# The attention loop of a Perceiver block in another order: TensorE takes Wo behind the keys and turns xn behind the values, and VectorE, ScalarE and POOL are reordered to match

## The reference

```python
def _L0_attn_ref(x, wq, bq, wk, bk, wv, bv, wo, bo):     # x is layer-normed
    q = proj(wq, bq); k = proj(wk, bk); v = proj(wv, bv)   # 16 heads of 16
    scores = jnp.einsum('bhqd,bhkd->bhqk', q, k) / np.sqrt(hd)
    attn = jax.nn.softmax(scores, axis=-1)
    o = jnp.einsum('bhqk,bhkd->bhqd', attn, v)
    align = jnp.sum(o * v, axis=-1, keepdims=True) / (v_norm_sq + EPS)
    o = o - align * v                                      # what lies along v is taken off
    return jnp.einsum('bsd,ed->bse', o, wo) + bo
...
x = x + _L0_xattn_ref(_layernorm(x), ctx_768, ...)
x = x + _L0_attn_ref(_layernorm(x), ...)
x = x + _L0_ffn_ref(_layernorm(x), ...)                    # argmax of 14 logits picks the expert
```

## Time and profile before

| what | us |
|---|---|
| median of 3 runs | 520.83 |
| lowest and highest | 520.41, 521.19 |
| the profiled execution | 520.4 |
| its span, first to last instruction | 518.4 |
| TensorE busy | 500.3 (97%) |
| VectorE, ScalarE busy | 344.8, 346.8 (67%) |
| POOL busy | 241.5 (47%) |
| granted TensorE clock, mean | 0.994 |

### The profile page before, as it was taken

How to read it: one execution, slowest core, us unless ns; L and a number is a source line. 1 busy time by engine, 2 the same in 40 slices (tenths; PEclk the granted TensorE clock), 3 DMA queues, 4 the chain that set the end, 5 groups by cost and what they waited for, 6 DMA issues and landing times.

```text
span 518.4 us, 14286 instructions
## 1 busy us (share of the span) xinstructions
PE 500.3 (97%) x4324; PEld 397.8 (77%) x4325; DVE 344.8 (67%) x1022; ACT 346.8 (67%) x837; POOL 241.5 (47%) x406
## 2 busy tenths in 40 slices
PE   8999999999999999999999999999999999999993
PEld 6554555566788788887878888778989999999992
DVE  4578666646788988898898989997553333323231
ACT  3777777668988888889888888887453334343430
POOL 2366555336434555564555546552753333333332
PEclk9999999999999999999999999999999999999997
DMA  8964446200001122212231111146667766666620
GB/s 299 368 198 150 157 157 209 63 1 1 2 3 38 45 86 93 92 54 84 93 91 50 58 61 60 45 135 206 191 200 236 215 216 204 224 182 216 192 82 10
DMA packets 30497, 65.68 MB, mean 127 GB/s; under 512 B 4640, under 2 KB 18594, under 8 KB 30448
## 3 DMA queue, kind: packets, MB, share of 16 engines
q1 hardware_dynamic: 26560, 55.99, 34.6%
q0 software_dynamic: 3456, 8.85, 4.4%
q10 hardware_dynamic: 432, 0.26, 0.2%
HBM read 54.21 MB, written 11.60 MB: 127 GB/s over the span
## 4 chain that ended last, share of the span: by engine, by line
PE 86%; DVE 5%; issue 4%; ACT 1%; POOL 1%; DVEq 0%; ACTq 0%; POOLq 0%
PE psum L1387 12%; PE psum L1400 11%; PE psum L1322 9%; PE psum L1273 6%; PE psum L1160 6%; PE psum L1281 5%; PE psum L1335 5%; PE psum L1294 5%; PE psum L1241 5%; PE psum L1203 3%; PE psum L1210 3%; PE psum L1172 3%; PE psum L1186 3%; PE psum L1214 3%; PE psum L1175 3%
## 5 line engine op out<-in xcount | busy, mean ns | idle before, releaser
L1387 PEld LDWEIGHTS psum<-arena,ring 128*128 128x128 f32 x640 | 77.3, 192 | 3.5 <-issue 1.7
L1387 PE MATMUL psum<-arena,ring 128*128 128x128 f32 x640 | 78.2, 275 | 0.9 <-ACT arena L1104 0.7
L1400 PE MATMUL psum<-w_s,arena 128*128 x320 | 75.9, 381 | 0.0
L924 DVE TENSOR_TENSOR arena<-psum,tok 128x256 f32<-128x256 f32 x40 | 17.0, 424 | 84.9 <-PE psum L1400 83.2
L1098 ACT ACTIVATE arena<-psum 128x256 f32<-128x256 f32 x40 | 15.4, 385 | 85.9 <-PE psum L1160 58.7
L1400 PEld LDWEIGHTS psum<-w_s,arena 128*128 128x128 f32 x320 | 57.8, 190 | 6.4
L483 POOL TENSOR_TENSOR ov<-o_n,v_s 128x256 f32<-128x256 f32 x32 | 23.5, 733 | 74.9 <-DVE o_n L693 74.9
L1068 ACT ACTIVATE arena<-kT,head_mask 128x256 f32<-128x256 f32 x128 | 57.4, 500 | 0.0
L541 POOL DMA_INDIRECT out<-arena,token_of x40 | 40.0, 999 | 19.0 <-POOL token_of L533 13.9
L1104 ACT ACTIVATE arena<-psum,b_s 128x128 f32<-128x128 f32 x160 | 45.6, 375 | 4.0 <-PE psum L1387 2.2
L795 DVE TENSOR_REDUCE smax<-psum 128x16 f32<-128x1024 f32 x32 | 39.1, 1221 | 4.8 <-PE psum L1294 4.4
(11 more groups left out here) (193 smaller groups left out, 1119.9 us busy)
## 6 DMA issues: line engine op xcount, KB each, us to landing
ring<-w SPq DMA_DIRECT2D x40, 512.0 KB, 3.7
w_s<-ctxT SPq DMA_DIRECT2D x15, 768.0 KB, 4.6
w_s<-w SPq DMA_DIRECT2D x16, 448.0 KB, 3.6
slot_rec<-routed SPq DMA_DIRECT2D x40, 132.0 KB, 3.5
tok<-x SPq DMA_DIRECT2D x16, 256.0 KB, 4.8
routed<-pad_rec SPq DMA_DIRECT2D x1, 1980.0 KB, 10.7
tok<-b SPq DMA_DIRECT2D x14, 128.0 KB, 3.0
out<-arena,token_of POOLq DMA_INDIRECT x40
```

The lines of the kernel that those rows point to most:

```text
L1387: mm = pe.matmul(hid_bank(p)[:, f * P:(f + 1) * P], w1_s[:, r, c * F + f * P:c * F + (f + 1) * P], xgT[:, p, c * P:(c + 1) * P], start=c = ...
L1400: mm = pe.matmul(bank(2 + q, D), hidT[:, q, f * P:(f + 1) * P], w2_s[:, bass.ds(e * (FC * D) + f * D, D)], start=f == 0, stop=f == FC - 1)
```

## The change

TensorE's step becomes: keys, Wo of tile `w`, queries, turn the probabilities, values, turn xn, scores, weighing, turn the output. Wo moves from the end of step `i - 1` to behind the keys of step `i`. Its tile is the same, and so is what it waits for. xn is turned between values and scores, where it stood between weighing and Wo, and the output is turned last. These are rows of a step of TensorE in the loop, first before, then after. `xnT,wk_s` are the keys, `xnT,wq_s` the queries, `av_s,xnT` the values, `arena,qT` the scores, `arena` 64x34 the weighing.

POOL adds the bias between `ov` and `along`, and in the loop `settled` comes ahead of `along`. ScalarE copies the queries ahead of the probabilities, and a step's end becomes: first half of the values, `oT`, the exponential, second half of the values. The diff, its core:

```diff
@@ gpsimd attention_step
                     pool.tensor_tensor(ov[:, :], o_n[:, :], v_s[:, (k - 3) % 4, :], ALU.mult).then_inc(s["ov_ok"], 1)
+                if live(i):
+                    need(pool, s["xn_ok"], i + 1)
+                    pool.tensor_tensor(rows(i), rows(i), bo_s[:, :], ALU.add).then_inc(s["bo_added"], 1)
+                if not isinstance(x, int):
+                    settled(x, (k - 9) % RING)
                 if live(y):
                     need(pool, s["coef_ok"], y + 1)
...
-                if not isinstance(x, int):
-                    settled(x, (k - 9) % RING)
-                if live(i):
-                    need(pool, s["xn_ok"], i + 1)
-                    pool.tensor_tensor(rows(i), rows(i), bo_s[:, :], ALU.add).then_inc(s["bo_added"], 1)
@@ scalar attention_step
-                if live(v):
-                    copy_probabilities(v, p)
-                if live(z) and k % GROUP == 0:
-                    route_exponents(z)
                 if live(i):
                     need(act, s["s_psum"], i - 1)
...
                     last.then_inc(s["q_ok"], 1)
-                if live(y):
-                    copy_output(y, (k - 3) % 2)
+                if live(v):
+                    copy_probabilities(v, p)
+                if live(z) and k % GROUP == 0:
+                    route_exponents(z)
...
                     spread_keys((2, 3)).then_inc(s["kd_ok"], 1)
                 if live(u):
+                    spread_first_values(u, (k - 1) % 2, (k - 1) % 4)
+                if live(y):
+                    copy_output(y, (k - 3) % 2)
+                if live(u):
                     exponentiate(u, (k - 1) % 2)
                 if live(u):
-                    spread_values(u, (k - 1) % 2, (k - 1) % 4)
+                    spread_second_values((k - 1) % 2, (k - 1) % 4)
@@ tensor attention_step
                 if isinstance(i, int) and i == NT:
                     before_scores()
                     all_scores()
+                    need(pe, s["l1_ok"], i)
+                    project(w, p)
                     return
...
                     need(pe, s["xT_ok"], i + 1)
                     need(pe, s["q_ok"], i)
...
+                    project_tile(wk_s, 0)
+                if live(w):
+                    need(pe, s["l1_ok"], i)
+                    project(w, p)
+                if live(i):
+                    project_tile(wq_s, 1).then_inc(s["qk_psum"], 1)
                 before_scores()
...
-                if ramp:
+                if live(t):
                     need(pe, s["xn_ok"], t + 1)
                     need(pe, s["xT_ok"], t)
+                    need(pe, s["oT_ok"], w + 1)
                     turn(bank(5), xn[:, 1 - p, :], s["xT_psum"])
                 if live(v) and ramp:
                     turn_probabilities(v, p)
                 all_scores()
-                if live(y):
-                    need(pe, s["xT_ok"], i + 1, NT)
-                    turn_output(y, (k - 3) % 2)
...
                     weigh_values(v, p)
-                if live(t) and not ramp:
-                    need(pe, s["xn_ok"], t + 1)
-                    need(pe, s["xT_ok"], t)
-                    need(pe, s["oT_ok"], y + 1)
-                    turn(bank(5), xn[:, 1 - p, :], s["xT_psum"])
                 if live(y):
-                    need(pe, s["l1_ok"], i + 1, NT)
-                    project(y, (k - 3) % 2)
+                    need(pe, s["xT_ok"], i + 2, NT)
+                    turn_output(y, (k - 3) % 2)
```

More of the change, by code:

```diff
@@ L701, in attention_step @@
                     dve.tensor_reduce(lmax[:, :], logit[:, :, :], AX.X, ALU.max).then_inc(s["lmax_ok"], GROUP)
+                if "weighing" in aside:
+                    aside["weighing"]()
                 if live(w):
                     need(dve, s["stats3_raw"], w + 1)
[L705 to L711, removed]
[L712 to L716 removed]
+                if live(y):
+                    need(dve, s["ov_ok"], y + 1)
+                    dve.tensor_reduce(dot[:, :], ov[:, :].rearrange("p (h d) -> p h d", h=NH), AX.X, ALU.add)\
+                        .then_inc(s["dot_ok"], 1)
+                if gather:
+                    need(dve, s["lmax_ok"], of_group)
+                    dve.tensor_tensor(lc[:, :, :], logit[:, :, :], each(lmax[:, :]), ALU.subtract)\
+                        .then_inc(s["lc_ok"], GROUP)
+                if live(y):
+                    need(dve, s["dot_ok"], y + 1)
+                    need(dve, s["rvv_ok"], y + 1)
+                    dve.tensor_tensor(coef[:, :], dot[:, :], rvv[:, (k - 3) % 4, :], ALU.mult).then_inc(s["coef_ok"], 1)
+                if settle:
+                    need(dve, s["ranked_ok"], of_last)
+                    dve.tensor_reduce(rank[:, :], ranked[:, :, :], AX.X, ALU.add).then_inc(s["rank_ok"], GROUP)
                 if scales:
@@ L725, in attention_step @@
                         .then_inc(s["ranked_ok"], GROUP)
-                if gather:
-                    need(dve, s["lmax_ok"], of_group)
-                    dve.tensor_tensor(lc[:, :, :], logit[:, :, :], each(lmax[:, :]), ALU.subtract)\
-                        .then_inc(s["lc_ok"], GROUP)
                 if sums:
@@ L775, in attention_step @@
                         .then_inc(s["pos_ok"], GROUP)
+                if gather:
+                    need(dve, s["cand_ok"], of_group)
+                    dve.tensor_reduce(arg[:, :], cand[:, :, :], AX.X, ALU.min).then_inc(s["arg_ok"], GROUP)
                 if shares:
@@ L778, in attention_step @@
                     dve.reciprocal(rec[:, done, R_PROB], lsum[:, :]).then_inc(s["prob_ok"], GROUP)
+                if live(u):
+                    need(dve, s["vv_ok"], u + 1)
+                    dve.tensor_reduce(vvsum[:, :], vv[:, :, :], AX.X, ALU.add).then_inc(s["vvsum_ok"], 1)
+                if gather:
+                    need(dve, s["arg_ok"], of_group)
+                    dve.tensor_tensor(onehot[:, :, :], experts, each(arg[:, :]), ALU.is_equal)\
+                        .then_inc(s["onehot_ok"], GROUP)
+                if live(t) and not (isinstance(t, int) and t in (1, 2)):
+                    normalise(t, (k + 1) % 2)
+                if isinstance(i, int) and i == 0:
+                    normalise(2, 0)
+                if isinstance(i, int) and i == -1:
+                    normalise(1, 1)
+                if live(w):
+                    dve.bn_aggr(rec[:, r, R_MEAN:R_MEAN + 2], stats3[:, :]).then_inc(s["stats3_ok"], 1)
+                if live(y):
+                    need(dve, s["along_ok"], y + 1)
+                    need(dve, s["oT_psum"], y - 1)
+                    dve.tensor_tensor(o_f[:, (k - 3) % 2, :], o_n[:, :], along[:, :], ALU.subtract).then_inc(s["of_ok"], 1)
                 if live(i):
```

86 lines of the change are left out of this document (33 added, 53 removed).

## The result

| what | before | after |
|---|---|---|
| median, us | 521.01 (6 runs, 520.33 to 521.52) | 532.90 (6 runs, 531.67 to 535.03) |
| ratio to before | | 1.0236, 95% interval 1.0221 to 1.0252 |
| profiled execution, its span | 520.4, 518.4 | 533.59, 531.7 |
| granted TensorE clock, mean | 0.994 | 0.992 |

The changed kernel is 2.4% slower, 532.9 us where 531.0 (524 to 535) was forecast. On the page of after, TensorE's busy time is 3.6 us more than in the earlier trace rows; VectorE's and ScalarE's hardly move, POOL's is 2.6 less. So of the 13.3 us, 9.7 are idle time of TensorE.

The account below looks back on a forecast made before the run. TensorE, busy 97% of the span, was taken as the bound. Added waits of 14.8 us less 4.5 and 0.2 removed made it net 10.1 us slower: 530.5, with the median 0.4 higher 531 us, range 524 to 535.

Parts of the forecast that it names:

- The `o_f` waits go: TensorE's nine waits for VectorE's `o_f` in the whole run all vanish: minus 4.5 us.
- xn becomes the bound: TensorE waits for VectorE's late xn: 2.0, 8.0 and 1.3 us in steps 4-11, loop, 28-29; expected sign 25 to 30 places.
- By kind of step: Loop waits for xn: 0.13 us in ordinary steps (k = 2), 0.60 in gather steps (k = 3), 0.69 at k = 0, 0.58 at k = 1.
- rival 2: At k = 1 POOL's `along` goes ahead of xn: 0.45 us more in each of four steps; 534 us, chance 0.16.
- VectorE waits out POOL's instruction: An xn beside POOL's `along` ends only behind it, about 4.46 instead of 4.24 us on the step's clock.
- A change of order removes none of these: TensorE's own work in an attention step, 7.30 us, stays; reordering only removes or makes waits.
- The loop and the steps written out: Added waits for xn: 8.0 us in loop tiles 12 to 27, 2.0 in steps 4 to 11, 1.3 in 28 and 29.
- Step 30: The slot plan delays x3, so values wait 1.1 us and xn 1.0 more: 2.1 in place of 1.3.
- The end: Last step's scores wait 1.0 us more for tile 30's shifted scores, plus 0.4 for Wo(28) being later: 1.4 added.
- The ramp stays: Ahead of the loop, the first probabilities still wait for the same exponential, so nothing is added.
- Priced at nothing: Waits for the exponential (covered by 0.3 us) or oT, and POOL's moved bias addition, were taken to cost nothing.
- Rival 4: A wash: waits for xn come to a third, 4 us, cancelling the `o_f` gain; 521 us, chance 0.04.

Follow-up runs that it names:

- a1_xn_early: Changed kernel with VectorE forming xn right behind the wait for the statistics, ahead of `dot` and the routing: 521.98 us, ratio to before 1.0021.
- b2_along_thin: Changed kernel with POOL forming only one column of 16 per head of `along`, so results differ from the reference: 537.03 us, ratio to before 1.0163.
- a3_fill: Changed kernel with seven unread matmuls added in the pause ahead of the scores of tile 31: 540.35 us, ratio to before 1.0215.
- a2_end: Changed kernel with Wo of tile 28 ahead of the scores again in the last attention step: 539.24 us, ratio to before 1.0213.
- a4_pool_old: Changed kernel with POOL's old order, `along` ahead of the `settled` waits and bias addition: 535.26 us, ratio to before 1.028.
- c0_after: Changed kernel without any edit, run again as partner on a chip where the kernel before took 528.24 us: 541.43 us, ratio 1.0259.
- b3_turn_later: Changed kernel with TensorE turning xn behind the scores instead of ahead of them: 525.25 us, ratio to before 1.0093.

## Why the prediction was right, point by point

- *The `o_f` waits go.* Right: no wait for `o_f` stands among those of after. One of them brought nothing: the wait of 1.0 among the slots was made over to the probabilities' copy and oT (0.40 and 0.29), and the slots lost another 0.44 in place of winning 1.0. The rest of that wasn't followed.
- *xn becomes the bound.* Right: 11.3 us in 20 places of up to 0.8 where the terms came to 12.3 in 23 and the marks said 25 to 30. One of the 20 lies in step 2, which the prediction didn't price; the four at k = 2 in the loop are too short for the list. But the list and the terms count differently. From due times, as the terms are, xn is late by 13.6 in steps 4 to 29 where the terms there came to 11.3. a1_xn_early shows the cause by the time: its ratio is 0.0215 lower, 11 us, when xn alone is moved. Between the two profiled executions it is 13.3 us, of them 10.9 in steps 4 to 29 and 1.1 from the keys of tile 31 to the first slot, where its clock didn't fall.
- *By kind of step.* Steps take, by their keys, 7.3 to 7.4, 7.9 to 8.1, 7.9 to 8.1 and 8.1 to 8.2 us for k = 2, 3, 0 and 1; the forecast was 7.4, 7.9, 8.0, 7.9. At k = 1 I had xn start ahead of `along`. It starts 0.10 behind (242.23, 242.33): rival 2's mechanism. Over the loop k = 1 is late by 3.65 us (0.85 to 0.97 a step) where 2.3 was forecast; the other three kinds together by 5.97 where 5.7 was. I had taken 0.3 for POOL's waits; `rec` ends at 242.10 and `along` starts 0.13 later. On the step's clock TensorE turns xn at 243.05 - 237.71 = 5.34; the forecast had 5.05, rival 2 5.50, among other things since TensorE starts 0.05 behind the end of xn's row and not 0.15. Against that, x3 starts 2.00 to 2.25 behind the keys in the loop and not 1.96.
- *VectorE waits out POOL's instruction.* Right. xn takes 0.40 alone and 0.68 beside `along`, and 0.40 again when `along` is short (b2_along_thin). The Trainium skill's rule, "SBUF — State Buffer", section "SBUF: two separate sides", that the first of the two has the shared port pair for the whole instruction, agrees with these rows.
- *"A change of order removes none of these."* It removed 0.1 us a step: 7.2 in place of 7.30 without waits, 2.0 us over steps 4 to 29. The prediction had no term for it.
- *The loop and the steps written out.* +6.46, +2.02 and +1.20 against 6.1, 2.0 and 1.3: the nearness is luck. xn was 2.3 us later than the terms, and the shorter steps took 2.0 of it back. Nor does the median's place between 531 and rival 2's 534 speak for that rival's sum: it would give the loop 8.0 + 1.8 + 1.4 - 1.9 = +9.3.
- *Step 30.* The mechanism was right, the values waited 0.76 for `logit` and xn 0.74, but its terms were 1.1 and 1.0. The slot plan takes 2.02 us in after (341.05 to 343.07), not the 2.38 taken from before.
- *The end.* The term furthest off: 1.1 forecast (1.4 less the `o_f` wait of 0.3), 2.93 measured. One part is size. The pause cost 358.18 - 356.17 - 0.37 = 1.64 where I had 1.0, because I let the maximum start 0.07 behind the scores. They end at 353.72 + 1.02 = 354.74, but VectorE, which first had the expert slots' tables to make (350.15 to 351.39), is not through with its gather step and starts the maximum 0.82 later:

```profile
355.56 1.21 DVE L794 TENSOR_REDUCE smax<-psum 128x16 f32<-128x1024 f32 x1
```

  The larger part was missing from the sum: behind the pause TensorE ran at 1.2 GHz. From Wo to the first slot it took 3.78 us; in a1_xn_early, at the full clock, 347.74 to 349.85, 2.11. That is 1.67 us. The two, less the waits of 0.26 and 0.21 that before has there, give 2.84 of the 2.93. That idle time brings the fall about is only supported (a3_fill, a2_end), and when it does stays open (below). The fall belongs to the profiled execution. Two other executions of after, at 532.57 and 532.82, were granted 0.996 on average, as much as b2_along_thin, whose clock fell nowhere before its last matmul. The fall alone takes 3.8 x 0.45 / 531.7 = 0.003 off the mean, so they ran without it, and they are only 0.1 to 0.3 below the median: how much of the 1.67 the median holds isn't shown, and it needn't be much.
- *"The ramp stays."* It didn't: in step 3 the probabilities wait 0.69 for the exponential and start 1.74 behind the queries where before it was 1.22. No oT stands ahead of this exponential yet. It waits 0.16 for its shifted scores, which start 0.51 later than before (130.20, 129.69) because the scores do; 0.24 of that is a wait for xn in step 2. With what the keys gained there the ramp cost 0.20.
- *Priced at nothing.* POOL's new order was rightly no loss (a4_pool_old: 2.4 us of waits more without it). The exponential's cover of 0.3 held only because the steps had grown longer: with xn in time it breaks in 7 places (2.1 us). The prediction called itself wrong if a wait for the exponential or for oT appeared. Both did, once each (0.69 in step 3, 0.29 among the slots), though in no step of the loop.
- *Smaller slips.* Before, TensorE turned xn 6.0 us after its keys by the prediction's own parts, and not 5.5; nothing in the sum used it. Rival 4 left out 2.5 us that it doesn't remove, 1.1 for the values in step 30 and 1.4 at the end: it would give about 523 and not 521.

Of the 13.3 us, then, 9.7 arose in steps 4 to 30, where the waits for xn and `logit` less the `o_f` waits stand, and 2.9 at the end. The forecast was 3.2 us low for the profiled executions (10.1 against 13.3): 1.8 at the end, 1.4 among the slots, and the rest nearly cancels. On the median it was 1.9 low. That this is about what the end was undersized by proves nothing, since the median need not hold the fall of the clock.

## What to carry to other kernels

An order for the busiest engine sets a due time for each result it reads. Write these times down, and then order the engines that supply them by due time: here the change gave xn 2.67 us in place of 6.0 and put it last on VectorE, and moving that one instruction gave back 11 of the 12 us. Check a forecast by its parts: here two sums came out near because an undersized loss met a gain that nobody had priced. An instruction whose waits come from another chain (POOL's four waits ahead of `along`) belongs behind what the bound engine needs, and a pause of the bound engine may cost more than its length.

## What the hardware showed that I had not expected

Behind the same pause of 1.57 us, with nearly the same work around it, TensorE's clock fell in some executions and not in others. In the profiles of after, c0_after and a4_pool_old Wo behind it takes 2.07 to 2.17; in those of a1_xn_early, b3_turn_later and b2_along_thin 1.18. In after the granted clock was 0.54 to 0.56 for some 3.8 us and it cost 1.67 us, as much as the pause. The fall doesn't come at once: the scores directly behind the pause ran at the full clock in after (1.09) and took 1.35 in c0_after and 1.60 in a4_pool_old. From 130 us on, the 12 profiles have 16 pauses of TensorE of 1.47 us and more before its last matmul. All six falls came right behind one of them or, in the longest, near its end: pauses of 1.57, 1.57, 1.57, 2.02, 2.07 and 3.50 us; behind the other ten, of up to 2.07, the clock stayed.

Where the pause was filled with matmuls that do nothing, the clock stayed. That is one profile, and three profiles with the pause unfilled kept it too. The mean clocks of the other executions don't decide it either. Of the six of each kernel, c0_after never had more than 0.993 and a3_fill had 0.995 or 0.996 in four, but b2_along_thin, with the pause unfilled, had 0.995 or 0.996 in five.
